# Weights once per layer, and the products with v in four parts between early projections

## The chip, the cores and the metric

The kernel runs on one core of a Trainium2 chip. The time is device microseconds of one execution, as a median over runs. TensorE (PE), VectorE (DVE), ScalarE (ACT) and GpSimd (POOL) compute; SyncE (SP) issues the DMA transfers.

## The reference

A batch of 4 sequences of 1024 tokens by 128 goes through one causal attention with a layer norm, then through six layers of windowed attention and a gated FFN, and a last norm. Of a layer (`rot` stands for the rotary step with its scale):

```python
def layer(x, Wqkv, qs, ks, Wo, g, bln, W1, b1, W2, b2):
    q, k, v = split(shift_tokens(x) @ Wqkv, 3)          # 16 heads of 64
    q, k = rot(l2norm(q) * qs), rot(l2norm(k) * ks)
    # each window of 32 queries sees its own and the window before (64 keys)
    p = softmax(mask(q @ k.T * 8))
    x = (p @ v) @ Wo + x
    h = (norm(shift_tokens(x)) * g + bln) @ W1 + b1
    a, gate = split(h, 2)
    return (a * gelu(gate)) @ W2 + b2 + x
```

## The kernel before, in words

`build` calls `clear_first_rows`, `mla_attention`, `local_layers` and `closing_norm`. The change lies in `local_layers` (L135 to L982) alone, and everything below is about it.

The work unit is a pair of 128-token tiles (256 tokens). A sequence has `POS` = 4 pairs, a layer `BATCH` = 4 sequences, called rounds; `f` counts the rounds over all layers, 24 of them, `p` the pair in a round. One step handles one pair in each of several stages at once: the projections q, k, v of pair `t` (`now`), the attention of pair `t-1` (`back1`), the product with Wo of `t-2`, the FFN of `t-3`, and ahead of time the first four projections of pair `t+1` (`project_next`, `EARLY` = 4). `rounds` (L238) writes the 16 steps of the first layer out, then a loop over layers 1 to 5 with a body of 16 steps, then three steps to drain.

Each engine has its own list of instructions, written out by hand in `step` of its block, and the engines meet at semaphores. TensorE fills PSUM banks from two rings of three: `bank_d` (L208) is emptied by VectorE, `bank_a` (L209) by ScalarE. `fill_a` and `fill_d` wait until the bank's last content has been taken.

- TensorE, end of a step (L578 to L592): `transpose_x`, `times_v(…, 0)`, projections 0 and 1 of the next pair, `times_v(…, 1)`, projection 2, `ffn_down` (L520), projection 3, transposes of y2 (L500). `times_v` (L428) multiplies the softmax weights with v for eight of the 16 heads: 64 small products in 64x64 tiles (each takes two passes in fp32), into two banks, after a matmul of two columns (L435). A projection (L413) is one matmul of 128x128 by 512, two passes.
- ScalarE (L710 to L723): `copy_attnT` (L661) empties those two banks, `square` (L614) squares an early projection for the norms.
- VectorE: `rotate` (L787) multiplies an early or late projection with the rotary table and frees its bank, `variances` and the softmax steps lie between.
- GpSimd: `add_products` (L910), `inverse_norms`, `norm_qk`, `normalise`, and at the end of a step `make_table` (L894), which makes the rotary table of pair `p` for round `f+1`.
- SyncE: `load_xs`, x1 out and in (L341, L349), three copies of v shifted by 32 rows (`v_back`, L361 to L363, 1 MB in all), x2 out (L369), and the weights, which are loaded again in every round `f` even where the layer is the same: w_qkv in two parts in step `p` = 3 (L338, L366), the rows of q and k scales in `p` = 0 (L335), w_o in `p` = 1 (L353), the FFN's in `p` = 2 (L373).

```python
                if runs(back1):
                    times_v(s, back1, 0)
                project_next(0)
                project_next(1)
                if runs(back1):
                    times_v(s, back1, 1)
                project_next(2)
```

Of the kernel before, what the change touches and what calls it, by code (L numbers as in the profile page):

```python
# [27 lines left out]
INNER = HEADS * DH  # L28
# [72 lines left out]
class Step:  # L101


    def __init__(self, f, p):
        self.f, self.p = f, p
        self.t = POS * f + p
# [5 lines left out]
class Pair:  # L112


    def __init__(self, step, lag):
# [3 lines left out]
        self.f = step.f + q // POS  # L119
        self.n = step.t - lag  # L120
# [3 lines left out]


def layer_of(f):

    return (f // BATCH) % DEPTH
# [6 lines left out]
def local_layers(nc, x_dram, x1_dram, w):  # L135
# [5 lines left out]
    with ExitStack() as ctx:  # L141
# [96 lines left out]
        def rounds(eng, step_fn, last_fn=None):  # L238


            for b in range(BATCH):
                for p in range(POS):
                    step_fn(Step(b, p))
            with nc.Fori(1, DEPTH, engines=[eng.engine], hint_back_edge=True) as layer:
                for b in range(BATCH):
                    for p in range(POS):
                        step_fn(Step(BATCH * layer + b, p))
            for t in range(PAIRS, PAIRS + MAX_LAG):
                step_fn(Step(ROUNDS, t - PAIRS))

        def prev(s):

            return Step(s.f, s.p - 1) if s.p else Step(s.f - 1, POS - 1)
# [24 lines left out]
        def _(sp):  # L278
            def load_w_qkv(f, lo, hi, done):
                sp.dma_start(w_qkv[:, lo:hi], w["Wqkv"][bass.ds(layer_of(f), 1), :, lo:hi]  # L280
                             .rearrange("one k n -> (one k) n")).then_inc(done, 16)

            def load_qk_rows(f):
                sp.dma_start(qk_row[:, :, :], w["qk_rows"][bass.ds(layer_of(f), 1), :]
                             .rearrange("one (r d) -> one r d", d=DH).to_broadcast([P, 4, DH])).then_inc(qkrow_in, 16)

            def load_wo(f):
                sp.dma_start(w_o[:, :, :], w["Wo"][bass.ds(layer_of(f), 1), :, :]
                             .rearrange("one (c k) n -> k (one c) n", k=P)).then_inc(wo_in, 16)

            def load_ffn(f):
                layer = bass.ds(layer_of(f), 1)
# [19 lines left out]
            load_xs(Step(0, 0).pair(0))  # L312
# [6 lines left out]
            def step(s):  # L319
# [31 lines left out]
                if runs(back2) and s.p == 1 and in_rounds(s):  # L351

                    load_wo(s.f)  # L353
                if runs(now):
# [9 lines left out]
                    if s.p == POS - 1:  # L364

                        load_w_qkv(s.f + 1, 2 * INNER, 3 * INNER, wv_in)  # L366
                if runs(back3):
# [3 lines left out]
                    if s.p == 2 and in_rounds(s):  # L371

                        load_ffn(s.f)  # L373
# [6 lines left out]
        def _(pe):  # L380
# [21 lines left out]
            def project(s, i):  # L402

                a, kind, c = chunks[i]
                if i == 0:
                    if s.p == POS - 1:
                        pe.wait_ge(wqk_in, 16 * (s.f + 2))
                    pe.wait_ge(a_free, ring_a.at(s, "xT")[1] + 1)
                if i == 8 and s.p == 0:
# [1344 lines left out]
```

## Time and profile before

| what | before |
|---|---|
| median of 3 runs | 4658.14 us (4657.95 to 4670.21) |
| the profiled execution's own time | 4670.98 us |
| its span, first to last instruction | 4669.2 us |
| mean granted TensorE clock | 0.959 |
| TensorE busy | 89% |
| DVE / ACT / POOL busy | 62% / 56% / 60% |
| the six layers | from about 930 to 4562 us |

The page lists busy time by engine, the chain that ended last, and groups of instructions by line. The trace behind it is asked for more: who waited for whom, and the instructions in order of time. The granted clock is the TensorE clock that the chip gave, as a share of 2.4 GHz. A busy TensorE includes matmuls whose ends are modelled.

### The profile page before, as it was taken

How to read it: one execution, taken by the hardware profiler on the slowest of the kernel's cores; microseconds unless marked ns; L12 is line 12 of the kernel's file. 1: busy time of each engine (PE TensorE's matmuls, PEld its weight loads, DVE VectorE, ACT ScalarE, POOL GpSimd, SP SyncE). 2: the span in 40 equal slices, each digit the busy share in tenths (PEclk: the TensorE clock that was granted, in tenths of full speed). 3: DMA queues.
4: the chain of work that ended last, by engine and by line, in shares of the span. 5: the costliest groups of instructions: out<-in, count | busy, mean ns of one | idle time of the engine just before them, and what ended most of it. 6: DMA issues, size and time to landing. Idle time of an engine off the chain costs nothing. (4 is left out here: it accounts for less than half of the span.)

```text
span 4669.2 us, 162098 instructions
## 1 busy us (share of the span) xinstructions
PE 4135.5 (89%) x67078; PEld 2766.5 (59%) x67078; DVE 2915.5 (62%) x4217; ACT 2616.0 (56%) x4417; POOL 2805.6 (60%) x3584
## 2 busy tenths in 40 slices
PE   5879788689999999999999999999999999999994
PEld 2434344346666666666666666666666666666663
DVE  5565656466666666666666666666666666666664
ACT  2545353446666656656656566566665656656552
POOL 0000000177777777777777777777777777777771
PEclk8989798889999999999999999999999999999997
DMA  0000000112222222222222223222222222222223
GB/s 28 3 15 2 15 2 15 41 39 65 65 70 74 58 68 67 72 55 67 66 70 64 56 68 79 62 59 70 68 72 55 65 66 70 64 56 67 70 64 81
DMA packets 284568, 258.77 MB, mean 55 GB/s; under 512 B 122871, under 2 KB 258508, under 8 KB 271148
## 3 DMA queue, kind: packets, MB, share of 16 engines
q1 hardware_dynamic: 283820, 248.14, 20.0%
q8 instruction: 550, 9.01, 0.9%
q14 instruction: 198, 1.62, 0.1%
HBM read 117.63 MB, written 29.77 MB: 32 GB/s over the span
## 5 line engine op out<-in xcount | busy, mean ns | idle before, releaser
L787 DVE TENSOR_TENSOR products<-bank_d,table 128x1024 f32<-128x1024 f32 x772 | 938.1, 1216 | 684.4 <-ACT sq L614 679.7
L910 POOL TENSOR_TENSOR products<-products 128x2048 f32<-128x2048 f32 x192 | 871.0, 4536 | 313.8 <-DVE products L787 313.8
L413 PE MATMUL bank_d<-w_qkv,xT 128*128 128x512 f32 x1544 | 807.5, 626 | 18.7 <-issue 13.0
L614 ACT ACTIVATE sq<-bank_d 128x512 f32<-128x512 f32 x772 | 468.0, 606 | 469.9 <-PE bank_d L413 457.4
L947 POOL TENSOR_TENSOR qk_rot<-products,rnorm 128x2048 f32<-128x2048 f32 x192 | 695.6, 3623 | 14.0 <-POOL rnorm L929 12.7
L785 DVE TENSOR_REDUCE ss<-sq 128x16 f32<-128x1024 f32 x386 | 468.8, 1214 | 229.3 <-ACT sq L614 229.3
L874 POOL MEMSET ident<- 128x128 f32 x1 | 0.2, 205 | 915.1 <-POOLq L1064 915.1
L954 POOL TENSOR_TENSOR prob<-prob,inv_sum 128x1024 f32<-128x1024 f32 x192 | 365.4, 1903 | 307.3 <-DVE inv_sum L767 307.3
L1491 DVE TENSOR_REDUCE part_max<-s_max 128x1 f32<-128x512 f32 (+3 forms) x768 | 399.5, 554 | 152.2 <-PE s_max L1240 101.3
L478 PE MATMUL scores<-kT,qT 64*32 64x64 f32 x24576 | 430.4, 218 | 24.4 <-issue 24.4
L413 PE MATMUL bank_a<-w_qkv,xT 128*128 128x512 f32 x768 | 403.1, 607 | 49.7 <-ACT gate L669 47.5
L1412 ACT ACTIVATE a_probT<-s_T 128x1024 f32<-128x1024 f32 x320 | 299.0, 938 | 249.6 <-PE s_T L1255 151.9
L478 PEld LDWEIGHTS scores<-kT,qT 64*32 64x32 f32 x24576 | 364.6, 107 | 116.3 <-issue 115.9
L661 ACT ACTIVATE attnT<-bank_a 128x512 f32<-128x512 f32 x384 | 208.5, 595 | 377.1 <-PE bank_a L445 377.1
L445 PE MATMUL bank_a<-probT,v 64*64 64x32 f32 x12288 | 381.1, 220 | 28.3 <-issue 28.1
L459 PE MATMUL bank_a<-ident,qk_rot 128*128 128x128 f32 x3072 | 382.9, 277 | 11.5 <-issue 5.8
L459 PEld LDWEIGHTS bank_a<-ident,qk_rot 128*128 128x128 f32 x3072 | 339.7, 141 | 84.9 <-issue 40.4
L445 PE MATMUL bank_a<-probT,v_back 64*64 64x32 f32 x12288 | 382.5, 221 | 4.0 <-issue 3.9
L650 ACT ACTIVATE prob<-prob 128x1024 f32<-128x1024 f32 x192 | 203.1, 1058 | 297.0 <-DVE prob L757 295.9
L445 PEld LDWEIGHTS bank_a<-probT,v_back 64*64 64x64 f32 x12288 | 333.4, 135 | 45.8 <-issue 44.0
L492 PE MATMUL bank_a<-attnT,w_o 128*128 128x256 f32 x1536 | 354.4, 384 | 6.7 <-issue 4.9
L766 DVE TENSOR_REDUCE row_sum<-prob 128x16 f32<-128x1024 f32 x192 | 233.2, 1215 | 196.8 <-ACT prob L650 196.8
(168 smaller groups left out, 7581.9 us busy)
## 6 DMA issues: line engine op xcount, KB each, us to landing
v_back<-v SPq DMA_DIRECT2D x96, 768.0 KB, 5.4
w_qkv<-in_Wqkv_dram SPq DMA_DIRECT2D x25, 1024.0 KB, 5.1
v_back<-v SPq DMA_DIRECT2D x192, 128.0 KB, 5.7
w_qkv<-in_Wqkv_dram SPq DMA_DIRECT2D x25, 512.0 KB, 5.4
xs<-x_layers SPq DMA_DIRECT2D x194, 64.0 KB, 2.1
w_o<-in_Wo_dram SPq DMA_DIRECT2D x24, 512.0 KB, 6.9
xr<-x_layers SPq DMA_DIRECT2D x96, 128.0 KB, 3.0
x<-x SPq DMA_DIRECT2D x96, 128.0 KB, 1.8
```

The source lines that it names most:

```text
L413: nc.tensor.matmul(bank[:, :], xT[:, P * a:P * (a + 1)], w_qkv[:, col:col + 512], start=True, stop=True).then_inc(d_filled if i < 8 else a ...
L445: last = nc.tensor.matmul(banks[u][64 * h2:64 * h2 + 64, col:col + 32], src[64 * u:64 * u + 64, a, DH * h:DH * (h + 1)], probT[ph][64 * u: ...
L459: last = nc.tensor.transpose(bank[:, P * j:P * (j + 1)], qk_rot[:, a, col:col + P], ident[:, :])
L478: last = nc.tensor.matmul(scores[row:row + 32, hp, u, :], qT[64 * h2:64 * h2 + 64, hp, 32 * win:32 * win + 32], kT[pair.par][64 * h2:64 * ...
L492: last = nc.tensor.matmul(bank[:, 0:PAIR], w_o[:, hp, :], attnT[:, hp, :], start=(hp == 0), stop=(hp == HP - 1))
L614: nc.scalar.activation(sq[j % 2][:, 8 * c:8 * c + 8, :], bank_d[slot][:, :].rearrange("p (h d) -> p h d", d=DH), ACT.Square).then_inc(squa ...
L785: nc.vector.tensor_reduce(ss[:, a, HEADS * kq:HEADS * (kq + 1)], sq[i // 2 % 2][:, :, :], AX.X, ALU.add)
L787: nc.vector.tensor_tensor(products[:, a, head:head + 8, :, :].rearrange("p h r (o d) -> p h r o d", o=2), bank[:, :].rearrange("p (h r d) ...
L910: link(nc.gpsimd.tensor_tensor(products[:, a, :, 0, :], products[:, a, :, 0, :], products[:, a, :, 1, :], ALU.add))
L947: nc.gpsimd.tensor_tensor(qk_rot[:, a, :].rearrange("p (h d) -> p h d", d=DH), products[:, a, :, 0, :], rnorm[:, a, 0:2 * HEADS].unsqueeze ...
L954: nc.gpsimd.tensor_tensor(prob[ph][:, :, :], prob[ph][:, :, :], inv_sum[:, ph, :].unsqueeze(2).to_broadcast([P, HEADS, 2 * WINDOW]), ALU.m ...
L1491: nc.vector.tensor_reduce(part_max[:, head, col:col + 1], s_max[m % 2][:, 0:width], AX.X, ALU.max).then_inc(max_free, 1)
```

## The change

1. `Step` and `Pair` carry the layer, the round in the layer (`b`) and `p`. Weights, the scale rows and the rotary table are loaded or made once per layer: w_qkv at the last pair of the last round (`b` = 3, `p` = 3) for the next layer, the scale rows at `b` = 0, `p` = 0, w_o at `b` = 0, `p` = 1, the FFN's weights at `b` = 0, `p` = 2, the tables in the four steps of `b` = 3. The waits on these loads follow.
2. `times_v` takes a range of its four head pairs. Each half is cut in two; behind each of the four parts stands one instruction group of other work: projection 0, 1, 2 of the next pair, and `ffn_down`.
3. ScalarE takes `square` 0 ahead of the first two copies of attnT, and `square` 1 and 2 ahead of the last two.

```diff
@@ SyncE @@
-                if runs(now) and s.p == 0:
-                    sp.wait_ge(table_ready, POS * (s.f + 1))
-                    load_qk_rows(s.f + 1)
-                if runs(now) and s.p == POS - 1:
+                if runs(now) and s.b == 0 and s.p == 0:
+                    sp.wait_ge(table_ready, POS * (s.layer + 1))
+                    load_qk_rows((s.layer + 1) % DEPTH)
+                if runs(now) and s.b == BATCH - 1 and s.p == POS - 1:
                     sp.wait_ge(d_filled, chunk_at(now, 7)[1] + 1)
-                    load_w_qkv(s.f + 1, 0, 2 * INNER, wqk_in)
+                    load_w_qkv((s.layer + 1) % DEPTH, 0, 2 * INNER, wqk_in)
...
-                if runs(back2) and s.p == 1 and in_rounds(s):
-                    load_wo(s.f)
+                if runs(back2) and s.b == 0 and s.p == 1 and in_rounds(s):
+                    load_wo(s.layer)
...
-                    if s.p == 2 and in_rounds(s):
-                        load_ffn(s.f)
+                    if s.b == 0 and s.p == 2 and in_rounds(s):
+                        load_ffn(s.layer)
@@ TensorE @@
-            def times_v(s, pair, half):
-                if half == 0:
+            def times_v(s, pair, half, first, last):
+                if half == 0 and first == 0:
                     pe.wait_ge(v_back_in[pair.par], 48 * (pair.k + 1))
-                banks = [fill_a(s, f"O{half}{u}", after="PT3") for u in range(2)]
-                nc.tensor.matmul(banks[1][:, 0:2], ident_b[:, :], ident_b[:, 0:2], start=True, stop=True)
-                for j in range(4):
+                if first == 0:
+                    banks = [fill_a(s, f"O{half}{u}", after="PT3") for u in range(2)]
+                    nc.tensor.matmul(banks[1][:, 0:2], ident_b[:, :], ident_b[:, 0:2], start=True, stop=True)
+                else:
+                    banks = [bank_a[ring_a.slots[f"O{half}{u}"]] for u in range(2)]
+                for j in range(first, last):
...
                 if runs(back1):
-                    times_v(s, back1, 0)
+                    times_v(s, back1, 0, 0, 2)
                 project_next(0)
+                if runs(back1):
+                    times_v(s, back1, 0, 2, 4)
                 project_next(1)
                 if runs(back1):
-                    times_v(s, back1, 1)
+                    times_v(s, back1, 1, 0, 2)
                 project_next(2)
+                if runs(back1):
+                    times_v(s, back1, 1, 2, 4)
                 if runs(back3):
                     ffn_down(s)
@@ ScalarE @@
+                square(new, 0)
                 if runs(back1):
                     copy_attnT(s, 0, 0)
                     copy_attnT(s, 0, 1)
-                square(new, 0)
                 square(new, 1)
+                square(new, 2)
                 if runs(back1):
                     copy_attnT(s, 1, 0)
                     copy_attnT(s, 1, 1)
-                square(new, 2)
@@ GpSimd @@
-                    make_table(s.f + 1, s.p)
+                    if s.b == BATCH - 1:
+                        make_table(s.layer + 1, s.p)
```

TensorE before, in the loop's body, from the end of the first half of the products with v to the start of the second (a register instruction prepares the value of a wait):

```order
L445 MATMUL bank_a<-probT,v 64x32 x4
L407 ISA
L408 REGISTER_ALU
L384 REGISTER_ALU
L413 MATMUL bank_d<-w_qkv,xT 128x512
L384 REGISTER_ALU
L413 MATMUL bank_d<-w_qkv,xT 128x512
L391 REGISTER_ALU
L435 MATMUL bank_a<-ident_b 128x2
L445 MATMUL bank_a<-probT,v_back 64x32 x4
```

TensorE in the changed kernel, at the end of the first of the four parts (L412 is the projection, L447 the products with v):

```order
L447 MATMUL bank_a<-probT,v 64x32 x4
L407 REGISTER_ALU
L383 REGISTER_ALU
L412 MATMUL bank_d<-w_qkv,xT 128x512
L447 MATMUL bank_a<-probT,v_back 64x32 x4
```

One projection follows the first quarter, and the small products go on behind it with no L435 between. The same piece stands behind the third quarter; behind the second stand a projection and L435, behind the fourth `ffn_down`.

ScalarE before, end of a step of the first layer:

```order
L630 ACTIVATE xT<-bank_a 128x256
L661 ACTIVATE attnT<-bank_a 128x8x64 x2
L614 ACTIVATE sq<-bank_d 128x512 x2
L661 ACTIVATE attnT<-bank_a 128x8x64 x2
L614 ACTIVATE sq<-bank_d 128x512 x2
```

ScalarE in the changed kernel, the same place:

```order
L637 ACTIVATE xT<-bank_a 128x256
L621 ACTIVATE sq<-bank_d 128x512
L668 ACTIVATE attnT<-bank_a 128x8x64 x2
L621 ACTIVATE sq<-bank_d 128x512 x2
L668 ACTIVATE attnT<-bank_a 128x8x64 x2
L621 ACTIVATE sq<-bank_d 128x512
```

A square moved ahead of each pair of copies.

The queue of SyncE before, from the FFN's weights of one round to the second part of w_qkv:

```order
L293 DMA w<-in_W_dram 128x682
L294 DMA w<-in_W_dram 128x2x128
L296 DMA w<-in_W_dram 85x128
L298 DMA small<-in_small_dram 128x9
L305 DMA xs<-x_layers 128x2x64
L306 DMA xs<-x_layers 128x2x64
L331 DMA xr<-x_layers 128x2x128
L280 DMA w_qkv<-in_Wqkv_dram 128x2048
L341 DMA x<-x 128x2x128
```

The changed kernel at the same place, in a round that loads no weights:

```order
L304 DMA xs<-x_layers 128x2x64
L305 DMA xs<-x_layers 128x2x64
L330 DMA xr<-x_layers 128x2x128
L340 DMA x<-x 128x2x128
```

The weights left the queue in three of four rounds; the other transfers kept their order.

## Rows read from the trace of the kernel before

**Rows 1.** The page, part 1: busy us (share of the span) xinstructions.
```profile
PE 4135.5 (89%) x67078; PEld 2766.5 (59%) x67078; DVE 2915.5 (62%) x4217; ACT 2616.0 (56%) x4417; POOL 2805.6 (60%) x3584
```

**Rows 2.** Waits of PE, 930 to 4562 us: total us, times, longest us.
```profile
PE bank_a L413 <- ACT gate L669: 47.5, 84, 0.6
PE bank_a L435 <- ACT v L626: 45.9, 95, 0.6
PE bank_a L423 <- ACT yT L696: 34.3, 65, 0.6
PE bank_a L445 <- issue: 32.0, 18, 3.5
PE scores L470 <- ACT kT L646: 27.4, 94, 0.3
PE scores L478 <- issue: 24.4, 21, 3.7
PE bank_d L413 <- issue: 13.0, 5, 3.2
```

**Rows 3.** Timeline of PE, one step: start us, us, op [idle before <-releaser].
```profile
2082.44 0.18 PE L435 MATMUL bank_a<-ident_b 128*128 128x2 bf16 x1 [0.47 <-ACT v L626]
...
2084.20 0.30 PE L445 MATMUL bank_a<-probT,v_back 64*64 64x32 f32 x8
2084.32 0.30 PE L445 MATMUL bank_a<-probT,v 64*64 64x32 f32 x8
2084.54 1.98 PE L413 MATMUL bank_d<-w_qkv,xT 128*128 128x512 f32 x4
2086.36 0.17 PE L435 MATMUL bank_a<-ident_b 128*128 128x2 bf16 x1
2086.46 0.32 PE L445 MATMUL bank_a<-probT,v_back 64*64 64x32 f32 x8
...
2088.46 1.12 PE L413 MATMUL bank_d<-w_qkv,xT 128*128 128x512 f32 x2
2089.42 1.46 PE L520 MATMUL bank_a<-gate,w 128*128 128x256 f32 x6
2090.72 1.02 PE L413 MATMUL bank_d<-w_qkv,xT 128*128 128x512 f32 x2
2091.58 0.38 PE L500 MATMUL bank_d<-ident,y2T 128*128 128x128 f32 x2
```

**Rows 4.** Timeline of POOL at the end of the same step.
```profile
2091.13 1.42 POOL L899 TENSOR_TENSOR table<-rotary,qk_row 128x256 f32<-128x256 f32 x2
2094.84 4.55 POOL L910 TENSOR_TENSOR products<-products 128x2048 f32<-128x2048 f32 x1 [2.30 <-DVE products L787]
```

**Rows 5.** Timeline of PE around four waits of the kind issue.
```profile
2314.30 0.30 PE L445 MATMUL bank_a<-probT,v 64*64 64x32 f32 x4 [2.84 <-issue]
...
2315.50 2.55 PE L520 MATMUL bank_a<-gate,w 128*128 128x256 f32 x6
...
2354.51 0.24 PE L445 MATMUL bank_a<-probT,v 64*64 64x32 f32 x2 [1.66 <-issue]
...
3773.55 1.28 PE L478 MATMUL scores<-kT,qT 64*32 64x64 f32 x37 [3.73 <-issue]
...
4381.94 1.28 PE L478 MATMUL scores<-kT,qT 64*32 64x64 f32 x37 [3.46 <-issue]
```

**Rows 6.** The page, part 3: queue, packets, MB, share of 16 engines.
```profile
q8 instruction: 550, 9.01, 0.9%
```

**Rows 7.** Timeline of the queue of SP: DMA issues.
```profile
2308.79 2.02 SPq L363 DMA_DIRECT2D v_back<-v  x1
...
3766.86 0.35 SPq L280 DMA_DIRECT2D w_qkv<-in_Wqkv_dram  x1
```

**Rows 8.** A stretch: us, busy PE, PEld, DVE, ACT, POOL, PEclk, DMA, GB/s.
```profile
2311.40:2319.00 7.60, 4.76 (x16) 3.11 (x14) 2.58 (x3) 2.13 (x4) 4.09 (x3) 0.78 0.18 43
```

**Rows 9.** Timeline of ACT in the step of rows 3.
```profile
2084.68 1.09 ACT L661 ACTIVATE attnT<-bank_a 128x512 f32<-128x512 f32 x2 [2.02 <-PE bank_a L445]
```

More of the change, by code:

```diff
@@ L101, with __init__ @@
 class Step:
-    def __init__(self, f, p):
-        self.f, self.p = f, p
-        self.t = POS * f + p
+    def __init__(self, layer, b, p):
+        self.layer, self.b, self.p = layer, b, p
+        self.f = BATCH * layer + b
+        self.t = POS * self.f + p
     def pair(self, lag):
@@ L119, in __init__ @@
         self.f = step.f + q // POS
+        self.layer = step.layer + (step.b + q // POS) // BATCH
         self.n = step.t - lag
@@ L363, in step @@
                     sp.dma_start(dst[0:q, 0, :], old[P - q:P, 1, :]).then_inc(done, 16)
-                    if s.p == POS - 1:
-                        load_w_qkv(s.f + 1, 2 * INNER, 3 * INNER, wv_in)
+                    if s.b == BATCH - 1 and s.p == POS - 1:
+                        load_w_qkv((s.layer + 1) % DEPTH, 2 * INNER, 3 * INNER, wv_in)
                 if runs(back3):
@@ L405, in project @@
                 if i == 0:
-                    if s.p == POS - 1:
-                        pe.wait_ge(wqk_in, 16 * (s.f + 2))
+                    if s.b == BATCH - 1 and s.p == POS - 1:
+                        pe.wait_ge(wqk_in, 16 * (s.layer + 2))
                     pe.wait_ge(a_free, ring_a.at(s, "xT")[1] + 1)
-                if i == 8 and s.p == 0:
-                    pe.wait_ge(wv_in, 16 * (s.f + 1))
+                if i == 8 and s.b == 0 and s.p == 0:
+                    pe.wait_ge(wv_in, 16 * (s.layer + 1))
                 bank = (fill_d if i < 8 else fill_a)(s, chunks[i])
@@ L444, in times_v @@
                                     h = 2 * hp + h2
-                                    last = nc.tensor.matmul(
+                                    ins = nc.tensor.matmul(
                                         banks[u][64 * h2:64 * h2 + 64, col:col + 32],
@@ L449, in times_v @@
                                         start=True, stop=True)
-                last.then_inc(a_filled, 2)
+                if last == 4:
+                    ins.then_inc(a_filled, 2)
             def transpose_qk(s, pair, i):
@@ L486, in times_wo @@
             def times_wo(s):
-                if s.p == 2:
-                    pe.wait_ge(wo_in, 16 * (s.f + 1))
+                if s.b == 0 and s.p == 2 and in_rounds(s):
+                    pe.wait_ge(wo_in, 16 * (s.layer + 1))
                 pe.wait_ge(a_free, ring_a.at(prev(s), "O11")[1] + 1)
@@ L524, in _ @@
             pe.wait_ge(constants_ready, INIT)
-            transpose_x(Step(-1, POS - 1))
+            transpose_x(Step(-1, BATCH - 1, POS - 1))
             for i in range(EARLY):
-                project(Step(-1, POS - 1), i)
+                project(Step(-1, BATCH - 1, POS - 1), i)
             def step(s):
@@ L559, in step @@
                 if runs(back3):
-                    if s.p == 3:
-                        pe.wait_ge(wffn_in, 64 * (s.f + 1))
+                    if s.b == 0 and s.p == 3:
+                        pe.wait_ge(wffn_in, 64 * (s.layer + 1))
                     ffn_up(s, "gA")
@@ L686, in step @@
                 if runs(back3):
-                    if s.p == 3:
-                        act.wait_ge(wffn_in, 64 * (s.f + 1))
+                    if s.b == 0 and s.p == 3:
+                        act.wait_ge(wffn_in, 64 * (s.layer + 1))
                     bank = filled(s, "xn")
@@ L775, in rotate @@
                 if i == 0:
-                    dve.wait_ge(table_ready, pair.n + 1)
+                    dve.wait_ge(table_ready, POS * pair.layer + pair.p + 1)
                 slot, n = chunk_at(pair, i)
@@ L829, in step @@
                 if runs(back3):
-                    if s.p == 3:
-                        dve.wait_ge(wffn_in, 64 * (s.f + 1))
+                    if s.b == 0 and s.p == 3:
+                        dve.wait_ge(wffn_in, 64 * (s.layer + 1))
                     hidden_units(s, "A")
@@ L892, in _, with make_table @@
             pool.wait_ge(constants_ready, INIT)
-            def make_table(f, p):
-                pool.wait_ge(qkrow_in, 16 * (f + 1))
+            def make_table(layer, p):
+                pool.wait_ge(qkrow_in, 16 * (layer + 1))
                 rows = slice(2 * p, 2 * p + 2)
```

36 lines of the change are left out of this document (18 added, 18 removed).

## The prediction

> **What bounds the kernel now.** I read the page first: TensorE is busy 4135.5 us (89% of the span), far ahead of every other engine [rows 1]. So the list of who waited for whom comes next, for TensorE alone, in the six layers (930 to 4562 us) [rows 2]. It shows two kinds of idle time. One recurs in nearly every step and waits for ScalarE (0.3 to 0.6 us each, 47.5, 45.9, 34.3 and 27.4 us in all). The other is "issue": TensorE waited for nothing that the profile knows, in the middle of a run of matmuls: 32.0 us in the products with v (L445), 24.4 us in the scores (L478), 13.0 us in the early projections (L413). The third view is the timeline of TensorE through one step [rows 3]: the end of a step is a small transposing matmul (L435), the first half of the products with v, two projections, the second half, one projection, the FFN's last product (L520), one projection. From 2082.44 to 2090.72 that is 8.28 us with no idle time between. Whatever is added to TensorE there is added to the step, 96 times, unless something later waits less for it.
>
> **Could a later wait absorb it?** The waits for ScalarE are loops that TensorE itself starts: ScalarE copies what TensorE has just filled. A later start of TensorE moves both. VectorE gets the early projections' squares sooner in the changed kernel, but the last of the four (behind L520) keeps its place, and the next step's GpSimd work waits for the product that follows it: 2.30 us idle before it [rows 4]. So I credit nothing for the earlier squares.
>
> **The sum, against this execution's 4671.0 us** (12.9 us above the median of 4658.1; the last term below accounts for most of that).
>
> *1. More changes between small and whole tiles.* The products with v use 64x64 tiles of the array, the projections the whole of it. Within L445 a group of eight starts every 0.12 us; from the last group to the projection it is 0.22 us, so 0.10 us is lost. The four projection passes then take 1.82 us, while two passes elsewhere take 0.86 us, so 1.72 for four: another 0.10 us [rows 3]. The same 0.10 appears for the two passes at 2088.46 (0.96 against 0.86). Leaving the small tiles for a whole-array matmul costs 0.20 us. Now it happens twice a step (before the projections behind each half); in four parts it happens four times (the fourth before L520). Two more exits: 0.40 us. The changed kernel also enters the small tiles twice more, straight from a projection, which no row shows. Nearest is L435 to L445, 0.10 us for a matmul of two columns [rows 3]; below, an entry may be free behind the projection's last pass. I take half of that range, 0.05, twice. 0.50 us a step in 96 steps is **+48 us**, between 38 and 58.
> The Trainium skill ("TensorEngine Tiling (Array Packing)", section Key Properties) says that a change of tiling mode drains the engine. By that rule an entry pays like an exit's first part, and the term would be 58 instead of 48; the exits' 0.10 agrees with it.
>
> *2. Waits for instructions in that stretch.* The "issue" waits lie in the middle of a group of equal matmuls (2314.30: 2.84 us, 2354.51: 1.66 us) [rows 5]. TensorE's program comes in pieces: 550 packets of queue 8 bring 9.01 MB, 16 KB each [rows 6]. At 2308.79 the third v_back copy was issued [rows 7], just before the 2.84 us. I read it as a piece queued behind 1 MB of v_back. There are 18 + 5 = 23 such waits in L445 and its projections, 45.0 us [rows 2]. The change moves them both ways. Gain: a projection (0.96 us) now stands ahead of the last quarter of the products, so a piece missed there is missed 0.96 us later and that work is already done; 18 x 0.96 = 17 us at most by this alone. Loss: the second and fourth parts come about 0.96 us later against the v_back transfer, so a piece that was asked for just before it may now fall behind it. In the 48 steps where the program's pieces end in those parts, I give that 4 chances in 10 at 1.66 us: 48 x 0.4 x 1.66 = 32. Together **+15 us**. Bounds: every one of the 23 goes, and with it the slow clock behind the long ones, 45 + 18 = -63 us (in the stretch of the 2.84 us wait the granted clock is 0.78, and L520 behind it takes 2.55 us instead of 1.46 [rows 3, 5, 8]; with the passes behind it I put 1.8 us on each of some ten long waits). At the other end all 48 get a wait, +80 us.
>
> *3. Weights once per layer.* 18 of 24 loads of w_qkv (1.5 MB by its shape), w_o and the FFN's weights (0.5 MB each) go, and on TensorE a few waits that cost nothing today: no row of the waits names a weight. What they cost is collisions with the instruction pieces: the 3.73 us wait in the scores at 3773.55 stands behind the w_qkv load of 3766.86 [rows 5, 7], and 3.46 us stands at the same place one layer later; with the slow clock (1.8 us each) that is 10.8: **-11 us**. Bounds: 0 if such a collision only moves to another transfer; -19 if five waits like that of 2354.51, in steps that load w_o ahead of v_back, go as well (they are among the 45.0 us of term 2). GpSimd's table (2 x 0.73 us in three of four rounds) was hidden: GpSimd idles 2.30 us right behind it [rows 4].
>
> *4. A new wait that I cost at nothing.* The third part needs the bank that ScalarE empties with attnT of the first half. Today two projections stand between, then one. Worked out from the timelines [rows 3, 9]: the first part starts 0.11 us after L435 and takes 0.94, exit 0.10, projection 0.96, so the second part starts at 2.1 to 2.2 and its last result is there at 3.3; ScalarE starts 0.06 us later and one copy takes 0.6 (two take 1.09): 3.96. TensorE arrives at 4.1. Cover 0.1 to 0.2 us; if it is gone, each 0.1 us costs 9.6 us.
>
> 4671.0 + 48 + 15 - 11 = **4723 us**, 1.4% above the median of before. (A difference under 0.3%, 14 us, can't be told from none here.)
>
> **The rivals.**
> *Starved less* (on the other side): the products with v are the densest instructions of the step, 256 instructions in 2.0 us [rows 3]; halved by a projection each time, a piece of 256 lasts 2.9 us. If that, together with fewer loads, lets every piece arrive, the waits of term 2 vanish: 4671 + 38 - 63 - 11 = 4635 us. It decides (the time falls below 4644) if at least 54 of those 63 us go. For it: the waits are long and recur at the same place each layer, so they have one cause. Against: the cause in my reading is v_back, which stays. Chance 0.12.
> *The exits are hidden*: weights are loaded ahead of the running matmul, the change costs no TensorE time, and term 2 comes to nothing: 4671 - 11 = 4660 us. Against: rows 3 show the 0.20 us in today's order. The Trainium skill ("TensorE: Matmul & The Clock Gate", section Architectural detail: the array is 16× 32×32, not 1× 128×128) says that the engine pulls weight loads ahead of running matmuls, which speaks for it; by that rule term 1 would be 0 and the time this 4660. Chance 0.08.
> *Starved more*: term 2 near its upper end, every second part now waits: 4723 + 60 = about 4783 us. For it: 48 chances against 18. Chance 0.17.
> *ScalarE late at the third part*: my cover of 0.1 us is wrong by 0.4: 96 x 0.4 = 38, 4761 us. Chance 0.10.
> *The change does not do what it says*: the loads leave and the parts stand in the new order on each engine, so that can't be.
>
> **How the numbers follow.** Forecast 0.53, the two slower rivals 0.27: slower 0.80. Same 0.08. Faster 0.12. The range goes from 4671 + 38 - 48 - 11 = 4650 (three quarters of term 2's lower bound), which leaves out the end of the fastest rival, to 4723 + 60 = 4783, which takes in the two slower ones: 4650 to 4785.
>
> **What the profile after would show.** Term 1: L435 to the projection behind the fourth part (8.28 us in a quiet step now) becomes 8.7 to 8.9; the passes behind each part stand 0.96 us apart where two follow. Term 2: "issue" waits in the products with v at other places; more of them if I am right, most gone if the first rival is. Term 3: no wait of over 3 us in the scores but at the end of a layer. Term 4: no row of L435 that waits for ScalarE's attnT. The forecast is wrong if this stretch stays near 8.3 us, or if it grows but "issue" falls by more than the growth.

## The result and the profile after

| | before | after |
|---|---|---|
| median | 4658.49 us (4657.95 to 4670.21, 4 runs) | 4751.91 us (4744.03 to 4756.52, 4 runs) |
| ratio, 95% interval | | 1.0188 (1.017 to 1.0207) |
| the profiled execution | 4670.98 us | 4748.0 us |
| granted TensorE clock | 0.959 | 0.960 |

The change makes the kernel 1.9% slower. The forecast said 4723 us, in a range of 4650 to 4785, with 0.80 on slower.

The page of the kernel after, parts 1 and 3. The columns are those of [rows 1] and [rows 6].

```profile
PE 4201.0 (89%) x67078; PEld 2772.0 (58%) x67078; DVE 2914.7 (61%) x4217; ACT 2619.6 (55%) x4417; POOL 2701.4 (57%) x3440
...
q8 instruction: 550, 9.01, 0.8%
HBM read 68.01 MB, written 29.77 MB: 21 GB/s over the span
```

The loads really left: HBM reads fell from 117.63 to 68.01 MB, and GpSimd has 144 instructions fewer. TensorE runs the same 67078 matmuls and is 65.5 us busier [rows 1]. I read it as matmuls behind a change of tile form that count as busy while they are held up. Its program still comes in 550 pieces.

Who TensorE waited for, in the layers of the kernel after (930 to 4640 us): us in total, times, longest us. It answers to [rows 2].

```profile
PE bank_a L447 <- issue: 64.3, 37, 2.6
PE bank_a L412 <- ACT gate L676: 50.1, 81, 0.6
PE bank_a L435 <- ACT v L633: 46.1, 95, 0.6
PE bank_a L422 <- ACT yT L703: 37.4, 72, 0.6
PE scores L473 <- ACT kT L653: 27.4, 94, 0.3
PE scores L481 <- issue: 14.2, 14, 1.6
```

The waits for ScalarE are what they were, to within 3.1 us a row. The waits for instructions in the products with v (now L447) rose from 32.0 us in 18 waits to 64.3 in 37; the five before an early projection (13.0 us) are gone; in the scores they fell from 24.4 us (longest 3.7) to 14.2 (longest 1.6).

The starts of ScalarE's copy of xT stand one step apart, so they give a step's length. The same stretch (1210 to 1290 us) of both traces, before and then after, all instructions that write xT on ScalarE:

```profile
L630 ACT ACTIVATE xT<-bank_a x3: 377/377/378, 1214.7 to 1288.1; 128x256 f32<-128x256 f32 x3
```
```profile
L637 ACT ACTIVATE xT<-bank_a x3: 378/378/378, 1214.0 to 1288.8; 128x256 f32<-128x256 f32 x3
```

Two steps took 73.4 us and take 74.8. To two decimals the undisturbed step went from 36.71 to 37.36 us, and the first layer of after has it eight times in a row. So **the quiet step grew by 0.65 us, 96 times: 62 us**. I call the remainder the *rest*: the sum of the last 92 steps less 92 quiet ones. It was 107.3 us and is 122.7 us, 15 us more. 62 and 15 make 77, which is what lies between the two profiled executions.

The timeline of TensorE after, from the end of a quiet half into a wait. It answers to [rows 3, 5]:

```profile
2092.74 0.18 PE L435 MATMUL bank_a<-ident_b 128*128 128x2 bf16 x1 [0.47 <-ACT v L633]
...
2093.69 0.30 PE L447 MATMUL bank_a<-probT,v 64*64 64x32 f32 x8
2093.92 1.13 PE L412 MATMUL bank_d<-w_qkv,xT 128*128 128x512 f32 x2
2094.97 0.32 PE L447 MATMUL bank_a<-probT,v_back 64*64 64x32 f32 x8
...
2099.70 0.29 PE L447 MATMUL bank_a<-probT,v_back 64*64 64x32 f32 x6
2101.51 0.19 PE L447 MATMUL bank_a<-probT,v_back 64*64 64x32 f32 x1 [1.52 <-issue]
...
2102.04 2.50 PE L523 MATMUL bank_a<-gate,w 128*128 128x256 f32 x6
```

From the last group of a part to the first of the next, over one projection, it is 1.28 us (2093.69 to 2094.97), where one group to the next is 0.12. The last wait stands in the fourth part, and L523 behind it takes 2.50 us in place of 1.46: the clock, which was granted at 0.50 (1.2 GHz) from 2102.5 to 2105.9 us and in full in the 9.8 us ahead. The two stretches of the same trace, before the wait and from it on (us, busy time by engine, granted clock, DMA share, GB/s):

```profile
2092.70:2099.70 7.00, 6.96 (x232) 4.64 (x236) 3.10 (x3) 2.86 (x6) 5.83 (x14) 1.00 0.67 171
2099.70:2105.00 5.30, 3.78 (x53) 2.81 (x47) 1.61 (x2) 1.74 (x4) 3.13 (x3) 0.77 0.02 3
```

What was TensorE waiting for? SyncE's queue, and the DMA packets of two stretches of one microsecond, 2098 to 2099 and 2099 to 2100, by queue (packets, MB, share of 16 engines):

```profile
2094.23 0.56 SPq L360 DMA_DIRECT2D v_back<-v  x1
2094.83 0.59 SPq L361 DMA_DIRECT2D v_back<-v  x1
2095.46 2.05 SPq L362 DMA_DIRECT2D v_back<-v  x1
```
```profile
q1 hardware_dynamic: 79, 0.24, 86.9%
q8 instruction: 1, 0.02, 8.5%
...
q1 hardware_dynamic: 35, 0.07, 37.8%
```

v_back's bytes fill the engines until about 2099; the piece comes in the tail of them, and TensorE goes on 2.5 us after its start. Putting the program's order beside the trace showed more: within one pass of the loop, the positions of these waits in TensorE's program lie **whole multiples of 256 instructions apart** (256 are 128 matmuls with their weight loads), and 256 are a piece of 16 KB at 64 B each. A piece is asked for when TensorE crosses into the one ahead of it; the table in the next section shows it. The Trainium skill ("Runtime: NRT & Kernel Launch", section Instruction fetch mechanics) says the same of the blocks, 256 instructions in 16 KiB. It also calls the cost of crossing one mostly hidden, and there this trace disagrees: 64.3 us in L447 alone.

### The profile page after: what moved, and what is told of

It reads as the page before. It is cut to its first block and busy times, and to the rows that moved or that the text cites. A ratio compares the mean times of both kernels' runs of the same rounds, so it can differ in the third digit from the quotient of the medians.

```text
span 4746.2 us, 161406 instructions
## 1 busy us (share of the span) xinstructions
PE 4201.0 (89%) x67078; PEld 2772.0 (58%) x67078; DVE 2914.7 (61%) x4217; ACT 2619.6 (55%) x4417; POOL 2701.4 (57%) x3440
## 3 DMA queue, kind: packets, MB, share of 16 engines
HBM read 68.01 MB, written 29.77 MB: 21 GB/s over the span
## 5 line engine op out<-in xcount | busy, mean ns | idle before, releaser
L412 PE MATMUL bank_d<-w_qkv,xT 128*128 128x512 f32 x1544 | 829.9, 630 | 5.9 <-DVE products L794 4.5
L447 PEld LDWEIGHTS bank_a<-probT,v_back 64*64 64x64 f32 x12288 | 331.8, 135 | 210.0 <-issue 206.7
L412 PE MATMUL bank_a<-w_qkv,xT 128*128 128x512 f32 x768 | 402.5, 606 | 52.1 <-ACT gate L676 50.1
L481 PE MATMUL scores<-kT,qT 64*32 64x64 f32 x24576 | 425.1, 218 | 14.2 <-issue 14.2
L447 PE MATMUL bank_a<-probT,v_back 64*64 64x32 f32 x12288 | 400.5, 223 | 37.1 <-issue 37.1
L447 PE MATMUL bank_a<-probT,v 64*64 64x32 f32 x12288 | 394.0, 220 | 27.3 <-issue 27.3
L447 PEld LDWEIGHTS bank_a<-probT,v 64*64 64x64 f32 x12288 | 334.6, 136 | 20.4 <-issue 20.4
```

The costliest lines, as they stand in the source:

```text
L412: nc.tensor.matmul(bank[:, :], xT[:, P * a:P * (a + 1)], w_qkv[:, col:col + 512], start=True, stop=True).then_inc(d_filled if i < 8 else a ...
L447: ins = nc.tensor.matmul(banks[u][64 * h2:64 * h2 + 64, col:col + 32], src[64 * u:64 * u + 64, a, DH * h:DH * (h + 1)], probT[ph][64 * u:6 ...
L481: last = nc.tensor.matmul(scores[row:row + 32, hp, u, :], qT[64 * h2:64 * h2 + 64, hp, 32 * win:32 * win + 32], kT[pair.par][64 * h2:64 * ...
```

## The experiments

Below, "quiet" and "rest" are worked out from the profiled run as above. The kernel before is 36.71 and 107, after is 37.36 and 123. The runs come in three sets: the two halves; the change of form, the small copies and v_back in two; v_back late and the moved pieces. The kernel before measured 4657.91, 4659.91 and 4664.35 us in them, so times of different sets compare to some 6 us. The ratios are to the kernel before of the same set.

### The two halves of the change, each alone

Weights once per layer, with both engines' order as before:

```diff
-                    times_v(s, back1, 0, 0, 2)
-                project_next(0)
-                ...
+                    times_v(s, back1, 0, 0, 4)
+                project_next(0)
+                project_next(1)
+                if runs(back1):
+                    times_v(s, back1, 1, 0, 4)
+                project_next(2)
```

> The changed kernel with the old order of the products with v and of ScalarE; weights once per layer stay. Theory (changes between small and whole tiles cost 0.65 us a step, the rest is waits for instructions behind v_back): 4640 to 4658 us, the quiet step 36.7 us as before, issue waits in the products with v near before's 32 us, no wait of over 3 us in the scores except at the end of a layer. Rival (loading once per layer shifts transfers so that more pieces of the program come late, whatever the order): 4690 us or more, with issue waits in the products of 60 us.

Measured 4681.91 us (4665.12 to 4715.43, 10 runs), ratio 1.0056 (1.0033 to 1.0078); quiet 36.71, rest 135. A miss: 50 MB fewer loads, and slower (0.6%, by its interval, and still under the rival's 4690 us). Its issue waits are 41.6 us in the products, 18.6 before an early projection and 7.7 before L523.

The four parts, with the weights loaded for every sequence as before:

> The kernel before with the products in four parts and the new ScalarE order; weights in every round. Theory: 4755 to 4775 us, quiet step 37.4 us, issue waits in the products 60 us or more. Rival (the weights are the slower half): 4720 us or less.

Measured 4786.48 us, ratio 1.0271 (1.0248 to 1.0294); quiet 37.36, rest 157. That is 11 us above the expected range. The quiet step is the full change's, so the 0.65 us are the parts' alone. The sum of the two halves (+24 and +128) is 152 us, the full change is +93: they do not add, and what does not add is the rest.

The full change with ScalarE's copies of attnT back ahead of the squares:

```diff
+                if runs(back1):
+                    copy_attnT(s, 0, 0)
+                    copy_attnT(s, 0, 1)
                 square(new, 0)
-                if runs(back1):
-                    copy_attnT(s, 0, 0)
-                    copy_attnT(s, 0, 1)
                 square(new, 1)
-                square(new, 2)
                 ...
+                square(new, 2)
```

> The changed kernel with ScalarE's old order: both copies of attnT ahead of square 0, both of the second half ahead of square 2. Theory: 4752 us within 6, quiet step 37.4 us; the order of ScalarE carries nothing, since squares are needed late. Rival (the new order delays the copy for which the third part waits): 4720 us or less.

Measured 4752.36 us, ratio 1.02 (1.0178 to 1.0222); quiet 37.37, rest 117. ScalarE's order is worth nothing.

Only the first half in parts:

```diff
                 project_next(1)
                 if runs(back1):
-                    times_v(s, back1, 1, 0, 2)
-                project_next(2)
-                if runs(back1):
-                    times_v(s, back1, 1, 2, 4)
+                    times_v(s, back1, 1, 0, 4)
+                project_next(2)
```

> The changed kernel with only the first half cut in two (square 2 back behind the copies of the second half). Theory: the quiet step is 37.0 to 37.05 us, half of the way, since one exit and one entry are added instead of two; time 4695 to 4720 us. Rival (the growth is the wait for a bank at the third part, not the tiles): quiet step 37.36 us, time 4740 us.

Measured 4808.64 us, ratio 1.0324 (1.0302 to 1.0346): the slowest of all, and a plain miss of my theory. The quiet step is as expected, 37.03 (half of the 0.65 us), but the rest is 204. Its issue waits in the products and before a projection, from 930 to 4600 us:

```profile
PE bank_a L447 <- issue: 82.0, 31, 3.6
...
PE bank_d L412 <- issue: 15.6, 5, 3.6
```

The cause shows when each crossing into a new piece is put beside the start of the transfers, in the third pass of the loop over layers (its 16 steps counted from 0). Times are us after the step's first L435, worked out from the traces; its piece is the start of the packet of 16 KB that answers crossing 1, and crossing 2 is where TensorE needs it. Stall is the distance of the two weight loads round the gap, some 0.25 us more than the idle time in the timelines:

```
kernel, step      v_back's bytes  crossing 1  its piece  crossing 2  stall
before, 6         2.4 to 7.8      1.6         2.7        5.4         none
before, 14        2.7 to 8.0      1.7         2.7        5.5         none
after, 14         2.7 to 8.2      2.9         6.1        7.0         1.8
after, 15         2.2 to 9.4      2.7         6.0        6.8         2.1
first half, 14    2.8 to 8.2      2.9         6.1        5.9         2.8
first half, 15    2.5 to 9.7      2.7         6.3        5.7         3.4
```

In the order of before, crossing 1 comes at 1.6 to 1.7 us and its piece goes out with the first of v_back's bytes. With a projection in the middle of the first half, crossing 1 comes 1.2 us later, behind v_back's start, and the piece waits until 6 us. With the second half in parts too, TensorE reaches the end of its piece 1.1 us later, so the stall is that much shorter. So the parts of the first half bring these stalls, and those of the second shorten them by 1.0 to 1.3 us. Over the layers, with weights once per layer in all three, the rest is 135 us undivided, 204 with the first half in parts and 123 with both: what the first half's parts add to the waits, the second half's take away again.

### The price of a change of form

```diff
                     ...
+                    if j == 1:
+                        nc.tensor.matmul(banks[1][:, 510:512], ident_b[:, :], ident_b[:, 0:2], start=True, stop=True)
```

> The kernel with weights once per layer and the order of the kernel before, with one more whole-array product (128x128 by 2 columns, into columns that are written again before they are read) in the middle of each half of the products with v. That gives the two extra changes of tile form of the full change, but moves no projection and no squares. Theory (the change of form is the price): the quiet step goes from 36.71 us to 37.3 to 37.4 us, as in the full change, and the time to 4735 to 4760 us. Rival (the price lies in the projections that were moved: their width, their banks, ScalarE's order behind them): the quiet step stays within 0.1 us of 36.71 and the time at 4680 to 4695 us.

Measured 4725.24 us, ratio 1.0148 (1.0128 to 1.0167); quiet 37.18, rest 100. Its timeline at the added matmul (L453), in the middle of the first half:

```profile
2085.71 0.30 PE L447 MATMUL bank_a<-probT,v 64*64 64x32 f32 x8
2085.94 0.18 PE L453 MATMUL bank_a<-ident_b 128*128 128x2 bf16 x1
2086.05 0.32 PE L447 MATMUL bank_a<-probT,v_back 64*64 64x32 f32 x8
2086.19 0.30 PE L447 MATMUL bank_a<-probT,v 64*64 64x32 f32 x8
```

From group to group it is 0.34 us where it is 0.12 without, and 0.02 more at the next group: 0.24 us for going out and in again round a matmul of two columns, 0.48 a step, and the quiet step grew by 0.47 to 0.48. The projections stayed where they were, so the rival falls. The step fell short of the expected 37.3 by 0.1, and the time of its range of 4735 to 4760 us by 10: the remaining 0.17 of the 0.65 us (0.08 for each) come with a projection in that place.

### Taking v_back's bytes away

```diff
-                    sp.dma_start(dst[q:P, :, :], src[0:P - q, :, :]).then_inc(done, 16)
-                    sp.dma_start(dst[0:q, 1, :], src[P - q:P, 0, :]).then_inc(done, 16)
-                    sp.dma_start(dst[0:q, 0, :], old[P - q:P, 1, :]).then_inc(done, 16)
+                    sp.dma_start(dst[q:q + 1, :, :], src[0:1, :, :]).then_inc(done, 16)
+                    sp.dma_start(dst[0:1, 1, :], src[P - q:P - q + 1, 0, :]).then_inc(done, 16)
+                    sp.dma_start(dst[0:1, 0, :], old[P - q:P - q + 1, 1, :]).then_inc(done, 16)
```

The same three issues at the same place, one row each. v_back is set to zero once at the start, so that the products read defined values; most of their terms from the window before are left out of the result. On the full change:

> The full change, with v_back's three copies cut to one row each (the products with v_back then use rows that are not this pair's). Theory (TensorE's next piece of program waits behind the bytes of v_back on the DMA engines): the issue waits of L447 fall from 64 us to under 15 us and the time from 4752 to 4685 to 4705 us, with the quiet step at 37.36 us still. Rival (the pieces come late for another reason: the number of DMAs on the queues, or their own length): issue waits of 50 us and more, and 4735 us or more.

Measured 4638.27 us, ratio 0.9958 (0.9941 to 0.9974), 114 us below after; quiet 37.36, rest **15**. Its waits of TensorE in the layers, the longest first:

```profile
PE scores L481 <- issue: 89.6, 296, 1.3
PE scores L481 <- ACT kT L653: 59.3, 96, 1.5
PE bank_a L412 <- ACT gate L676: 52.4, 86, 0.6
PE bank_a L435 <- ACT v L633: 46.1, 95, 0.6
```

L447 has no issue wait at all. (In this trace the records of the mask's small matmuls are incomplete, 66626 of 67078 in all, so the 0.3 us in which they ran reads as idle time in the scores, 296 times; the steps' length shows that it is none.) The theory holds and was too careful (47 us below its range): not only L447's 64 us but nearly all of the rest was v_back's bytes, the waits in the scores and the slow clock behind each stall included.

On weights once per layer:

> Weights once per layer with the order of the kernel before, and v_back's three copies cut to one row each. Theory: the 68 us of issue waits in the products with v and behind them (L447 41.6, L412 18.6, L523 7.7) go nearly all, quiet step 36.71 us: 4610 to 4640 us. Its time would also show that the excess over 4658 us of weights once alone was these waits. Rival (as above): 4665 us or more.

Measured 4589.04 us, ratio 0.9852 (0.9833 to 0.9871); quiet 36.70, rest 37, again below the expected range. The kernel before with small copies was not run, so what weights once per layer is worth without v_back's bytes stays open. The four parts cost 49 us by the medians where no bytes are in the way (46 by the profiled spans): 61 us by 92 quiet steps, less 22 of rest, and some 7 ahead of these steps and behind them. Halving the dense run of small matmuls does keep TensorE better fed, as one rival of the prediction had it (L447 still has 5.7 us of issue waits here, none in the version above), but it is a third of the price. Those 5.7 us are part of the 22; where the others lie was not followed up.

### Moving v_back's bytes

Half of v_back as soon as that half of v is written, ahead of SyncE's wait for y; only the other half at the old place; otherwise weights once per layer:

```diff
+                if runs(now):
+                    sp.wait_ge(a_free, ring_a.at(s, (0, "v", 1))[1] + 1)
+                    ...
+                    sp.dma_start(dst[q:P, 0, :], src[0:P - q, 0, :]).then_inc(done, 16)
+                    sp.dma_start(dst[0:q, 1, :], src[P - q:P, 0, :]).then_inc(done, 16)
+                    sp.dma_start(dst[0:q, 0, :], old[P - q:P, 1, :]).then_inc(done, 16)
                 if runs(back2):
                     sp.wait_ge(d_free, ring_d.at(s, "y")[1] + 1)
                     ...
-                    sp.dma_start(dst[q:P, :, :], src[0:P - q, :, :]).then_inc(done, 16)
-                    ...
+                    sp.dma_start(dst[q:P, 1, :], src[0:P - q, 1, :]).then_inc(done, 16)
```

> Weights once per layer with the order of the kernel before; v_back's copy of the first 128 rows' half of v and the two small copies are issued as soon as that half is written, ahead of SyncE's wait for y, and only the other half at the old place. Theory: the transfer that the next piece waits behind is half as long (about 3 us instead of 5.5 us), so the piece starts some 2.5 us earlier and stalls of up to 3 us shrink to about 0.5 us: 4620 to 4650 us, between the version with small copies and 4682 us. Rival (the halves collide with another fetch, or with the loads of xs, at the new place): 4670 us or more.

Measured **4627.40 us** (4620.93 to 4628.64), ratio 0.9925 (0.9909 to 0.9942); quiet 36.70, rest 58. That is the fastest here with v_back copied whole, 0.7% faster than before and 2.6% than after. Its issue waits in the products with v:

```profile
PE bank_a L453 <- issue: 16.2, 27, 1.6
```

All of v_back at the end of the step instead (SyncE's block moved behind the store of x2), on weights once per layer:

```diff
-                if runs(now):
-                    sp.wait_ge(a_free, ring_a.at(s, (1, "v", 1))[1] + 1)
-                    ...
                 if runs(back3):
                     sp.wait_ge(d_free, ring_d.at(s, "y2")[1] + 1)
                     ...
+                if runs(now):
+                    sp.wait_ge(a_free, ring_a.at(s, (1, "v", 1))[1] + 1)
+                    ...
```

> Weights once per layer, the order of the kernel before, and v_back's three copies whole but issued by SyncE at the end of the step (behind the store of x2) in place of ahead of it, some 10 us later, when TensorE is in the transposes of q and k and uses up its program slowly. Theory (it is the meeting of v_back's bytes with the next piece of program that costs): nearly as good as with small copies (4589 us): 4590 to 4610 us. Rival (the bytes cost the same wherever they are, or delay the loads of xs behind them): 4640 us or more.

Measured 4647.18 us (4639.18 to 4654.74, 10 runs), ratio 0.9958 (0.9939 to 0.9976); quiet 36.71, rest 73. Outside the theory's range and inside the rival's time, and yet neither holds: the late copies cost 58 us over small ones, where those at the old place cost 93. The issue waits in the products (L445 here) fell to 7.4 us, but others came, listed here:

```profile
PE bank_a L420 <- ACT yT L697: 48.5, 73, 1.1
PE bank_d L410 <- issue: 8.3, 8, 1.4
PE bank_a L410 <- DMA w_qkv<-in_Wqkv_dram: 7.4, 5, 1.8
```

The last is a side effect of my edit: the v part of the next w_qkv is loaded in the moved block and now comes late once a layer. On the kernel before that effect is four times as frequent:

> The kernel before with v_back's copies moved in the same way. Against the version above it gives what weights once per layer is worth when no piece of program meets v_back. Theory (the reloads cost next to nothing by themselves; their loss in the first run was a change of which pieces meet v_back): 4595 to 4625 us, 5 to 15 us above the version above. Rival (weights once costs time by itself): below the version above.

Measured 4749.49 us, ratio 1.0169 (1.0123 to 1.0215); quiet 36.72, rest 193. Outside what either expected, and it doesn't answer its question. Its waits say why:

```profile
PE bank_a L411 <- DMA w_qkv<-in_Wqkv_dram: 51.8, 23, 3.3
PE bank_a L421 <- ACT yT L694: 47.1, 62, 1.1
PE bank_a L421 <- POOL prob L952: 33.5, 21, 2.5
...
PE bank_a L443 <- issue: 9.1, 16, 1.9
```

23 waits of 2.3 us for w_qkv, and 21 for prob, where the trace of before has 3. With a reload for every sequence the moved load lies in the way; what weights once per layer is worth with v_back late, and the load left where it was, wasn't tried.

On the full change:

> The full change with v_back's copies moved in the same way. Theory: the quiet step of 37.36 us stays and the rest goes, 4640 to 4660 us, 45 to 60 us above the first of this set: the price of the four parts alone. Rival (the order in four parts keeps its waits for instructions): 4700 us or more.

Measured 4684.30 us (4678.19 to 4693.21, 10 runs), ratio 1.004 (1.0021 to 1.0058); quiet 37.37, rest 56. That is 68 us below after by moving bytes alone, and 37 us above the same with undivided halves (expected 45 to 60: again the parts' rest is smaller, 56 against 73, and takes some of the price back). It missed its range of 4640 to 4660 as the version on weights once per layer did.

### Moving the pieces

```diff
+            for _ in range(100):
+                pe.wait_ge(xs_in[0], 32)
             rounds(pe, step)
```

On weights once per layer. Of the 100 waits written, TensorE's program keeps 50 more instructions.

> Weights once per layer, order and v_back of the kernel before, with 50 more instructions (waits long fulfilled) on TensorE ahead of the layers, so that every piece of its program begins 50 instructions earlier in the loop. Theory (the stalls sit where a piece ends in the products with v): the stalls that were in steps 4, 5, 6 and 12, 13, 14 of the 16 come one or two steps sooner, at 3 to 5 and 11 to 13, and the time stays at 4670 to 4700 us, since the pieces drift through all places in 8 steps. Rival (the stalls belong to fixed steps, by what SyncE loads there): they stay in their steps.

Measured 4701.96 us (4692.67 to 4712.88, 10 runs), ratio 1.0085 (1.0065 to 1.0104); quiet 36.70, rest 143. The length over the quiet step in each of the 16 steps of the loop's body, median of its 5 passes, worked out from the xT copies and counted as in the table above:

```
step                    0   1   2   3   4   5   6   7   8   9  10  11  12  13  14  15
before                0.2 0.2 0.6 0.4 6.3 2.2 0.1 0.1 0.1 0.0 0.1 0.2 4.6 1.0 0.1 2.1
weights once          0.2 0.0 0.3 0.3 6.1 3.8 6.5 0.1 0.2 0.0 0.1 0.0 1.7 5.2 0.9 2.0
the same, 50 earlier  0.1 0.9 2.2 5.3 7.1 0.1 0.1 0.1 0.2 0.0 0.4 6.5 1.0 0.1 0.7 1.8
after                 0.1 0.0 0.2 0.2 4.3 1.7 3.7 3.4 0.1 0.0 0.1 0.0 0.9 2.6 3.6 2.9
v_back in two         0.2 0.0 0.2 0.3 4.0 0.7 1.4 0.0 0.2 0.0 0.1 0.0 0.6 1.6 0.6 2.1
```

The groups of long steps come eight steps apart, since a step is 5.12 pieces long and the crossings drift through all places in eight. 50 instructions moved both groups one to two steps sooner, as expected: where TensorE stalls is a matter of where its code lies. What it cost is not clear of the noise: 1.0085 (1.0065 to 1.0104) stands against 1.0056 (1.0033 to 1.0078) of another set, 14 us, and the rests differ by 8.

The second line against the first says where weights once per layer alone lost: in steps 5, 6 and 13. Two things differ there. The first is a load: before, SyncE issued that of w_o just ahead of v_back in one step of four (1, 5, 9, 13); the queue in step 5 of the first pass before, and in the same step with weights once:

```profile
1743.78 0.38 SPq L288 DMA_DIRECT2D w_o<-in_Wo_dram  x1
1744.28 0.56 SPq L361 DMA_DIRECT2D v_back<-v  x1
```
```profile
1735.15 0.55 SPq L360 DMA_DIRECT2D v_back<-v  x1
```

These steps' products began (first L435) at 1742.70 and 1734.16, so the first v_back issue moved from 1.58 to 0.99 us behind that. The large packets (v_back's) began at 4.3 to 4.6 us in step 5 and 4.5 to 5.2 in step 13, and with weights once at 2.2 to 2.6 and 3.0 to 3.5. In step 5, where crossing 1 stays at 1.8 to 1.9 us, its piece went out at 3.8 to 5.1 with that load, and without it at 5.1 to 5.7 in four passes and at 2.6 in one; TensorE's idle time there went from 0.8 to 1.9 us to 1.9 to 2.2 us, and none in the last pass.

The second is the place of the code. The edit changes TensorE's waits for loads, and with them the length of its program: counted in the traces, the borders of the pieces lie 6 to 12 instructions later in the steps of the loop with weights once per layer (7 in step 6, 11 in step 13); the four parts alone move none. The crossing ahead of crossing 1 moved by it from -5.4 to -4.5 us in step 6 and from -1.8 to -0.8 in step 13. The piece that follows started at -2.2 to -1.5 us before, and with weights once at 0.2 to 0.4 in three passes of step 6 and in all five of step 13. TensorE then stood 0.5 to 1.1 us at crossing 1, which came at 2.7 to 3.3 us in place of 1.6 (step 6) and 1.9 (step 13). As in the table of crossings that is late against v_back: the next piece started at 6.1 to 8.1 us, and TensorE stood again at crossing 2, for 1.8 to 2.8 us in seven of these eight passes. Before, the same piece started at 2.3 to 4.0 us.

In step 13 both differ; in step 6 no load ahead of v_back is left out. Which of them costs more over the whole is **not shown**: no run put the load alone back, and none moved the code alone by these few instructions. Step 12 became shorter.

## Why the prediction was right, by its steps

*Direction and size.* Slower, inside the range, 29 us above the forecast. 25 of them are in the sum: the profiled executions rose by 77 us where it had 52. The other 4 are the distance of after's profiled execution from its median. (By the medians the kernel lost 93 us, since the profiled execution of before lay 12.5 us above its own. That the prediction's last term accounts for most of this, as it says, no row shows.)

*Term 1, changes of form, +48 (38 to 58).* The right mechanism, undersized: 0.65 us a step, 62 us, just above its upper end. The step that failed is the entry: "I take half of that range, 0.05, twice". The way out is as the prediction had it, 0.23 us from the last group to the projection (2093.69 to 2093.92), but from there to the next group it is 1.05 us where a projection had 0.96, so the entry is 0.09, with 0.02 more at the group behind it. The added matmul says the same: 0.24 us for out and in round two columns and 0.08 more with a projection there, 0.32 in place of the 0.25 taken. The term would have been right to 4 us with the upper value of 0.10, which the Trainium skill's rule ("TensorEngine Tiling (Array Packing)", section Key Properties: a change of mode drains the engine) spoke for. The prediction looked for L435 to the projection behind the fourth part at 8.7 to 8.9 us; in the quiet steps of the trace it is 8.93.

*Term 2, waits for instructions, +15.* Right in kind, and by the waits themselves near in size: 45.0 us in 23 waits became 64.3 in 37, 19 us more. The rest holds terms 2 and 3 together, and there the prediction gave +4 where it rose by 15. That the 15 equals this term's 15 is chance, and the 4 chances in 10 behind the term came from no row. Both of its halves show in the crossings. The loss ("a piece that was asked for just before it may now fall behind it") is crossing 1 at 2.7 to 2.9 us instead of 1.6; the gain (a projection ahead of the last quarter) is the 1.1 us by which after's stalls are shorter than those with the first half alone in parts. Wrong was where the bounds came from: this term was reckoned for the products and their projections only, while the bytes of v_back cost 114 us in all, in the scores and by the clock too.

*Term 3, weights once, -11 (0 to -19).* Wrong for itself: alone it costs 24 us. The waits over 3 us in the scores did go, as expected, but the bound "if five waits like that of 2354.51, in steps that load w_o ahead of v_back, go as well" had a wrong cause. In the same step with weights once the wait stands without the load, at 1.92 us in place of 1.66. And the term left out that fewer waits in TensorE's program move the borders of its pieces by 6 to 12 instructions, after which TensorE stands in steps 6 and 13. Beside the four parts the same edit gained 35 us (4786.48 to 4751.91), and this isn't a constant of the edit: it depends on which pieces meet v_back. The 29 us by which the whole is off owe something to luck: the weights alone cost 24 us where this term gave -11 (35 off), the parts alone 128 where terms 1 and 2 gave 63 (65 off).

*Term 4, the bank behind attnT, 0.* Right: no row of L435 waits for attnT, and ScalarE's order made no difference (4752.36 against 4751.91). Its rival, *ScalarE late*, fell with it.

*The exits are hidden* fell with the quiet step. *Starved less* is half true, and its reason against it held: "the cause in my reading is v_back, which stays". With small copies the four parts do have 22 us less rest than undivided halves, but the price of form is 61. *Starved more* is what the parts do without weights once per layer (4786.48 us), and with the first half only (4808.64).

## What to carry to other kernels

TensorE's program is a stream with a deadline: where many small matmuls run (here 256 instructions in 3.8 us of a step), a large DMA issued in that stretch delays the next piece of program, and the wait shows up as "issue" at positions 256 instructions apart. Move or split the bytes rather than the arithmetic, and judge an edit that changes code length, order or small loads with such waits taken out, because otherwise some tens of us either way are luck of position: here the same edit cost 24 us in one order of the products and gained 35 in the other. A change between small tiles and the whole array costs about 0.24 to 0.32 us for out and in again, so in a kernel like this one whole-array work belongs between such runs and not in them.

## What the hardware showed that I had not expected

Removing 50 MB of loads made the kernel slower (1.0056, 1.0033 to 1.0078), with longer waits where pieces of TensorE's program met 1 MB of v_back. 50 instructions ahead of the layers moved both groups of stalls to other steps, and borders that lie 7 and 11 instructions later moved the crossing ahead of two stalls by 0.9 to 1.0 us. A stall of 1.52 us stands in a stretch of 5.3 us with a granted clock of 0.77, and the six passes of L523 behind it took 2.50 us instead of 1.46: these passes alone add 1.04 us to it.
